# Query and key preparation by quarters of the heads in two buffers, with joint transfers, a matmul mask for the maxima, and new orders

## The reference

```python
q = _rmsnorm((x @ Wq).reshape(B, T, H, D), q_rms_w)
k = _rmsnorm((x @ Wk).reshape(B, T, H, D), k_rms_w)
v = (x @ Wv).reshape(B, T, H, D)
omega_eff = softplus(omega) * slopes
gate = softplus(einsum('bthd,hd->bht', k, u_n) / sqrt(D))   # one factor per key and head
bias = -dist * omega_eff * gate            # dist = max(i - j, 0)
bias = where(causal, bias, -inf)
attn = softmax(q @ k.T / sqrt(D) + bias)
y = (attn @ v).reshape(B, T, H * D) @ Wproj
```

## Time and profile before

| | |
|---|---|
| median of 3 runs | 910.95 us (905.34 to 912.75) |
| the profiled execution | 906.46 us, span 904.7 us |
| mean granted TensorE clock of it | 0.954 |
| busy: PE, DVE, ACT, POOL | 784.6, 701.8, 652.3, 646.0 us |
| DMA bytes | 77.92 MB, 96,546 packets |

### The profile page before, as it was taken

How to read it: one execution, slowest core, us unless ns; L and a number is a source line. 1 busy time by engine, 2 the same in 40 slices (tenths; PEclk the granted TensorE clock), 3 DMA queues, 4 the chain that set the end, 5 groups by cost and what they waited for, 6 DMA issues and landing times.

```text
span 904.7 us, 25206 instructions
## 1 busy us (share of the span) xinstructions
PE 784.6 (87%) x9336; PEld 539.2 (60%) x9336; DVE 701.8 (78%) x2230; ACT 652.3 (72%) x1401; POOL 646.0 (71%) x746
## 2 busy tenths in 40 slices
PE   2548988898999999898998999998998899998974
PEld 1233755576666676576665776576665766575752
DVE  7868858786878879687876879787877879798933
ACT  5555857675996789766986879866986779863643
POOL 2523856687698868788697868889697868884761
PEclk9687999999999999999998999999999999999986
DMA  7033623647044711746054630746054720826330
GB/s 200 4 68 75 137 42 60 119 83 131 2 109 93 172 32 35 143 97 131 2 122 74 157 52 14 162 96 135 2 117 85 158 45 14 164 56 136 49 60 12
DMA packets 96546, 77.92 MB, mean 86 GB/s; under 512 B 72982, under 2 KB 83432, under 8 KB 96360
## 3 DMA queue, kind: packets, MB, share of 16 engines
q1 hardware_dynamic: 95912, 74.72, 40.6%
q10 hardware_dynamic: 512, 1.59, 0.8%
HBM read 5.29 MB, written 2.10 MB: 8 GB/s over the span
## 4 chain that ended last, share of the span: by engine, by line
PE 46%; SPq 13%; ACT 10%; DVE 9%; DMA 9%; issue 6%; POOL 5%; ACTq 0%; DVEq 0%; POOLq 0%
PE ps L955 10%; PE ps L957 9%; PE ps L956 9%; SPq L595 8%; PE ps L1059 5%; SPq L599 4%; PE ps L1074 3%; DMA y_hl<-ytt 3%; PE ps L1100 3%; PE ps L1101 3%; DMA k<-gtt 3%; ACT qkn L898 3%; DMA k<-qkn 3%; POOL qkn L777 3%; DVE junk L1359 2%
## 5 line engine op out<-in xcount | busy, mean ns | idle before, releaser
L753 POOL TENSOR_TENSOR pt_l<-pt 128x512 f16<-128x512 f32 x368 | 320.8, 901 | 112.7 <-ACT pt L928 112.6
L1359 DVE CUSTOM_DVE_ANT_0 junk<-ps,causal_row 128x512 f16<-128x512 f32 (+3 forms) x512 | 219.3, 486 | 46.5 <-PE ps L1074 45.3
L928 ACT ACTIVATE pt<-ps 128x512 f32<-128x512 f32 (+1 forms) x384 | 176.7, 527 | 71.0 <-PE ps L1102 46.4
L777 POOL TENSOR_TENSOR qkn<-qkn,rs 128x512 f32<-128x512 f32 x124 | 128.5, 1067 | 57.3 <-ACT rs L866 57.3
L1100 PE MATMUL ps<-q,k 128*128 128x512 f16 (+3 forms) x512 | 148.2, 302 | 1.0 <-ACT pt L928 0.7
L1101 PE MATMUL ps<-q,k 128*128 128x512 f16 (+3 forms) x512 | 147.5, 301 | 0.0
L955 PE MATMUL ps<-v_buf,pt 128*128 128x65 f16 x1280 | 131.8, 195 | 2.1 <-DVE ytok L1380 1.5
L1074 PE MATMUL ps<-k,q 96*128 96x512 f16 (+3 forms) x512 | 98.9, 306 | 38.9 <-DMA k<-gtt 24.8
L956 PE MATMUL ps<-v_buf,pt 128*128 128x65 f16 x1280 | 131.7, 194 | 0.0
L957 PE MATMUL ps<-v_buf,pt_l 128*128 128x65 f16 x1280 | 131.4, 194 | 0.0
L955 PEld LDWEIGHTS ps<-v_buf,pt 128*128 128x128 bf16 x1280 | 118.9, 98 | 14.4 <-issue 5.8
(11 more groups left out here) (178 smaller groups left out, 1994.6 us busy)
## 6 DMA issues: line engine op xcount, KB each, us to landing
q<-qkn SPq DMA_DIRECT2D x96, 256.0 KB, 5.2
k<-qkn SPq DMA_DIRECT2D x90, 256.0 KB, 5.9
x_in<-in_L_attn_x SPq DMA_DIRECT2D x8, 256.0 KB, 3.2
out<-x_out SPq DMA_DIRECT2D x8, 256.0 KB, 2.3
k<-qkn ACTq DMA_DIRECT2D x6, 256.0 KB, 8.2
k<-q SPq DMA_DIRECT2D x1, 1024.0 KB, 9.2
q<-nmt SPq DMA_DIRECT2D x64, 2.0 KB
y_hl<-ytt SPq DMA_TRANSPOSE x64, 3.3
```

Of the source, the lines that this page charges most:

```text
L753: g.tensor_tensor(pt_l[:, h % 2, c], pt[:, h % 2, c], pt_h[:, h % 2, c], ALU.subtract).then_inc(s_pt_l, 1)
L777: g.tensor_tensor(qk, qk, r.unsqueeze(3).broadcast_to([P, HH // 2, 2, D]), ALU.mult).then_inc(s_qkn, 1)
L928: a.activation(pt[:, h % 2, c], ps[:, j, 0:width], ACT.Exp).then_inc(s_exp, 1)
L1359: ins = d.tensor_tensor_reduce(junk[:, part.unit(s, i)[0], col:col + (ib + 1) * P], part.bank(s, i)[:, col:col + (ib + 1) * P], causal_row ...
```

## The change

1. **Quarters, two buffers.** `qk` is now (quarter `qd`, block `t`): one bank holds four heads of q and four of k. There are 16 such banks a batch as before, in two places of `qkn` of four heads each, used in turn; the whole is as large as before. `take_qk` waits for the transfers of the quarter before the last one only.
2. **Joint transfers.** `q1`, `k1` become one tensor `qk1` with, per quarter and odd or even heads, a block of k beside a block of q; `q2`, `k2` become `qk2`. The parts in `qkn` lie so that a transfer carries a q and a k block. A quarter takes 2 DMAs for the upper parts of `qk1`, 2 for the gate rows (four rows by two heads each), 4 for `qk2`. The bytes are the same, and so is the number of DMAs of a batch (32). Maxima wait for their quarter's first four DMAs. In batch 0 ACT issues the odd heads' part of quarters 0 and 1 (`place_odd_heads`), three 256 KB DMAs each.
3. **Mask by matmul.** Behind each of the four matmuls of a head's maxima PE adds the mask with a 128-column matmul; DVE takes the maximum with a plain `tensor_reduce` that negates and writes 16-bit numbers. `nm` turns and copies 16-bit numbers. The buffer `junk` is gone.
4. **Heads and weights.** Heads are computed in an order in which pairs are swapped (`pair_of`, `head_of`); Wq and Wk are loaded in 8 pieces so that the weights lie by quarters. The scale of the gate logits moves into two ACT instructions. POOL's `over_rms` waits once for two blocks, and does both of them, 16 of 512 elements a batch as before; in batch 0 DVE does the keys of quarters 0 and 1.
5. **New orders** on all engines, in all parts but `tail`.

```diff
-UNITS = {"m": 2, "h": 4, "out": 1, "qk": 2, "gl": 1, "gr": 1, "t": 2, "a": 3, "nm": 1, "v": 1, "wp": 1}
+UNITS = {"m": 2, "h": 4, "out": 1, "qk": 1, "gl": 1, "gr": 1, "t": 2, "a": 3, "nm": 1, "v": 1, "wp": 1}
...
+        def uses(b, qd):
+            return (b * 4 + qd) // 2 + 1
+        def place_upper(eng, qd, n):
+            eng.dma_start(qk1[0:D, qd, n, :, :, :], qkn16[n * D:(n + 1) * D, qd % 2, 1:3, :, :]).then_inc(s_upper[qd % 2], 16)
+        def place_lower(eng, qd, n):
+            eng.dma_start(qk2[D:P, qd, n, :, :, :], qkn16[n * D:(n + 1) * D, qd % 2, 0:2, :, :]).then_inc(s_low[qd % 2], 16)
+            eng.dma_start(qk2[0:D, qd, n, :, :, :], qkn16[n * D:(n + 1) * D, qd % 2, 2:4, :, :]).then_inc(s_low[qd % 2], 16)
...
+            def place_operands(part, s, b, qd):
+                both = range(1) if b == 0 and qd < 2 else range(2)
+                sp.wait_ge(s_hi, b * H + (qd + 1) * QH)
+                for n in both:
+                    place_upper(sp, qd, n)
+                part.taken(sp, ("gr", qd // 2, s[-1]))
+                for n in range(2):
+                    sp.dma_start(qk1[GROW:GROW + 4, qd, n, 0, :, :],
+                                 gtt[qd % 2 * 2 + n::4, :]).then_inc(s_gates[qd % 2], 16)
+                part.taken(sp, ("t", 2 * qd + 1, s[-1]), 1)
+                for n in both:
+                    place_lower(sp, qd, n)
...
+            def take_qk(part, s, b, qd, t):
+                if t == 0 and b * 4 + qd >= 2:
+                    act.wait_ge(s_upper[qd % 2], (uses(b, qd) - 1) * 32)
+                    act.wait_ge(s_low[qd % 2], (uses(b, qd) - 1) * 64)
...
             def max_scores(part, s, b, h):
-                pe.wait_ge(s_grow, (b * 2 + h // HH + 1) * 128)
+                pe.wait_ge(s_upper[qd % 2], uses(b, qd) * 32)
+                pe.wait_ge(s_gates[qd % 2], uses(b, qd) * 32)
...
-                        mm = pe.matmul(dst, q1[0:MROW, row(h), ib * P:keys], k1[0:MROW, row(h), 0:keys], start=True, stop=True)
+                        pe.matmul(dst, q1(h)[0:MROW, ib * P:keys], k1(h)[0:MROW, 0:keys], start=True, stop=False)
+                        mm = pe.matmul(dst[:, ib * P:keys], ident16[:, :], causal16[:, :], start=False, stop=True)
...
             def maxima(part, s, b, h):
-                        ins = d.tensor_tensor_reduce(junk[:, part.unit(s, i)[0], col:col + (ib + 1) * P], part.bank(s, i)[:, col:col + (ib + 1) * P],
-                                                     causal_row[:, T - (ib + 1) * P:T], 1.0, -3.0e38, ALU.add, ALU.max,
-                                                     negm[:, ib, column(h):column(h) + 1])
+                        ins = d.tensor_reduce(negm[:, ib, h:h + 1], part.bank(s, i)[:, col:col + (ib + 1) * P], AX.X, ALU.max,
+                                              negate=True)
...
             def take_max_rows(part, s, b, qd):
-                part.taken_by(d.tensor_scalar(nmt[:, :], part.bank(s)[0:QH, :], -1.0, None, ALU.mult), s)
+                part.taken_by(d.tensor_copy(nmt[:, :], part.bank(s)[0:QH, :].bitcast(F16)[:, 0:T]), s)
```

More of the change, by code:

```diff
@@ L489, in macaron @@
         s_out = sem("s_out")
-        s_dup = sem("s_dup")
-        s_low = sem("s_low")
-        s_grow = sem("s_grow")
+        s_upper = [sem(f"s_upper{i}") for i in range(2)]
+        s_low = [sem(f"s_low{i}") for i in range(2)]
+        s_gates = [sem(f"s_gates{i}") for i in range(2)]
         s_mrow = sem("s_mrow")
@@ L712, in _ @@
             for h, s in enumerate(slopes_of(H)):
-                last = g.memset(slopes[:, row(h):row(h) + 1], s)
+                last = g.memset(slopes[:, h:h + 1], s)
             last.then_inc(s_const, 1)
@@ L839, in gelu @@
                 act.preload_act_table_set(EXP_SET)
-            def take_qk(part, s, b, hf, t):
-                g = b * 2 + hf
-                if t == 0 and g > 0:
-                    act.wait_ge(s_grow, g * 128)
-                    act.wait_ge(s_dup, g * 64)
-                if t == TB // 2 and g > 0:
-                    act.wait_ge(s_low, g * 64)
-                blk = g * TB + t
-                for j in range(2):
-                    part.full(act, s, j)
-                    if blk >= 2:
-                        act.wait_ge(s_sqsum, (blk - 2) * 2 + j + 1)
-                    a.activation(sq[:, t % 2, j, :], part.bank(s, j), ACT.Square).then_inc(s_sq, 1)
-                    part.taken_by(a.activation(qkn[:, j, t // 2, :, (t % 2) * P:(t % 2 + 1) * P],
-                                               part.bank(s, j).rearrange("p (i n) -> p i n", n=P), ACT.Copy), s, j)
@@ L864, in inverse_rms, with two @@
+            def inverse_rms(part, s, b, qd, th):
+                n = (b * 4 + qd) * 2 + th + 1
+                def two(t):
+                    return t[:, :, qd % 2, 2 * th:2 * th + 2, :].rearrange("p j t m -> p j (t m)")
+                act.wait_ge(s_sqsum, n * 2)
+                a.activation(two(ssl), two(ss), ACT.Ln, bias=rms_eps[:, :],
                              scale=1.0 / (D * QKV_UP * QKV_UP)).then_inc(s_ssl, 1)
-                act.wait_ge(s_ssl, blk + 1)
-                a.activation(rs[:, t, :], ssl[:, t, :], ACT.Exp, scale=-0.5).then_inc(s_rs, 1)
+                act.wait_ge(s_ssl, n)
+                a.activation(two(rs), two(ssl), ACT.Exp, scale=-0.5).then_inc(s_rs, 1)
@@ L897, in hi_parts, with place_odd_heads @@
                     part.full(act, s, j)
-                    a.activation(qkn16[:, j, 0, p % 4, :], part.bank(s, j), ACT.Identity, scale=w[:, :]).then_inc(s_hi, 1)
-            def place_first_keys(part, s, b, hf):
-                if b + hf == 0:
-                    act.wait_ge(s_k1_zero, 16)
-                    act.wait_ge(s_hi, HH)
-                    place(act, k1[0:D, :, :], 0, 1, 0, s_grow)
-                    part.taken(act, ("gr", *s[1:]))
-                    for r in range(2, 4):
-                        place_gates(act, 0, r)
-                    place(act, k2[D:P, :, :], 0, 1, 0, s_dup)
-                    part.taken(act, ("t", 3, s[-1]), 1)
-                    place(act, k2[0:D, :, :], 0, 1, 1, s_low)
+                    a.activation(qkn16[:, p // 2 % 2, UPPER[j], p % 2, :], part.bank(s, j), ACT.Identity, scale=w[:, :]).then_inc(s_hi, 1)
+            def place_odd_heads(part, s, b, qd):
+                if b == 0 and qd < 2:
+                    if qd == 0:
+                        act.wait_ge(s_k1_zero, 16)
+                    act.wait_ge(s_hi, (qd + 1) * QH)
+                    place_upper(act, qd, 1)
+                    part.taken(act, ("t", 2 * qd + 1, s[-1]), 1)
+                    place_lower(act, qd, 1)
             def v_hi(part, s, b, j, t):
```

593 lines of the change are left out of this document (307 added, 286 removed).

## The result

| | before | after |
|---|---|---|
| median of the runs (lowest to highest) | 908.14 us (904.37 to 912.75) | 834.42 us (833.35 to 835.25) |
| ratio, 95% interval | | 0.9185 (0.9133 to 0.9238) |
| span of the profiled execution | 904.7 us | 833.3 us |
| mean granted clock | 0.954 | 0.975 |

Times are medians of the fast runs, and a ratio is always to the kernel before, measured beside the run in question. The changed kernel is 8.1% faster.

What follows compares the result with a forecast made beforehand. PE, busy 784.6 of 904.7 us, was taken as the bound, with idle time hanging on the `qkn` buffer wait. 906.5 + 28.7 - 6.4 - 12.2 - 12.0 - 4.1 - 7.3 - 3.0 - 2.0 = 888.2, plus 2: 890 us, range 868 to 914.

Steps and rivals of the forecast that it cites:

- PE "busy 93.6": First body at full clock: PE busy for 93.6 of 99.0 us, taken as work that counts in full.
- I let 3.0 us stand: Bodies: of 5.4 us idle PE in a full-clock body, 3.0 us stay, so -2.4 x 5 = -12.0 us.
- bound to one buffer that no longer exists: Bodies: the projection's wait behind the first half's transfers hangs on the single `qkn` buffer and goes with two.
- Masks, +28.7: PE, all batches: 512 mask matmuls of 128 columns at 0.056 us each add 28.7 us, nothing hidden.
- Turns, -6.4: PE: four turns of the maxima take 0.40 us in 16 bits against 0.60; 32 blocks save 6.4 us.
- Maxima on DVE, 0: DVE: plain reduction takes about 1.2 ns a column, as the fused mask and maximum does, so no change.
- lead -6.1: Kernel start: -4.1 us from half the 8.2 us wait before the first maxima, -2.0 from moving DVE's low weight parts.
- 115 to 249 -7.3: Stretch 115 to 249 us: 4.0 of 5.0 us gate-row waits and half of 6.7 us low clock go, -7.3 us.
- late -3.0: Behind the last body's start: of 3.3 us of gate-row waits, 3.0 us go.
- Slower: the waits only move: Rival, bodies: PE waits for DVE's maxima instead of DMA, nothing won there, 925 us; chance 0.15.
- Only the clock comes back: Rival, no change: long waits go, short ones take their place, 907 us; chance 0.20.
- Faster still: Rival: idle PE falls to 1 us a body, outside stretches lose remaining low clock and waits, 871 us; chance 0.18.

Runs made afterwards that it cites:

- the model of before's wait: Changed kernel, copies of quarters 0 and 2 waiting for both buffers' upper halves and their own lower halves: 902.8 us with old orders, 854.9 us with new orders.

## Why the prediction was right and wrong, step by step

- **The steps that failed, and their sizes.** The sum gave 888.2 us for the profiled execution, which took 835.25: 53 us less. Three steps account for it. PE "busy 93.6", with 2.8 us for masks less turns (and 0.3 because the stretch read was 99.0 us long and the period 99.3), stood as a floor of 96.7 us a body, and was 94.2: 12.5 us in five bodies. The idle PE left in a body, "I let 3.0 us stand", was 0.4: 13 us. And outside the five bodies the sum had -8.1 us where -35.9 were measured: 28 us. So the terms of gain were too small everywhere, while the price of the masks as PE's work was right.
- **What bounds the kernel.** That the wait of the earlier trace rows would go with the clock's falls was right: the clock is 1.00 in every body. That PE "busy 93.6" is work that stays was wrong. Dense time was 87.0 us, so up to 6.6 us of the busy time were gaps too short to be seen in it; after the change the same difference is 4.2 us (94.2 and 90.0), so some 2.4 of them went. The page Perfetto Trace Analysis of the Trainium skill (Identifying the Most-Contended Engine) says that busy time of matmuls is no good measure of the headroom, since matmuls are pipelined; the traces agree, by these 6.6 us, and the prediction did not weigh it.
- **Idle PE after: "I let 3.0 us stand".** It was 0.4. The excess fell from 14.8 to 4.6 us, 51 us in five bodies, where the forecast had 12.2 + 12.0 = 24.2. In the busy times, the mean body's idle PE fell by 6.3 us (101.75 less 95.03, to 0.4) and its busy time beyond the dense one by 3.8 (8.0 to 4.2). The forecast kept more than half of the idle time of a full-clock body and all of the short gaps; the reordering took away both. I had written that "a new order always has waits of its own", with no row behind it.
- **Buffers as the cause.** The prediction gave the gain to the buffer ("bound to one buffer that no longer exists"). By the model of before's wait it is worth 4.6 us in the old orders; the new orders are worth 48 to 64 us, and they had no term of their own in the sum.
- **Masks, +28.7.** Right as PE's work (a mask's step is 0.056 us, the dense time grew by 22.9 us in all, and doubled masks cost 23.0), but their price in time depends on the kernel: in the kernel before, masks and turns together cost 3 us, where PE had 14.8 us of excess a body, and in the changed kernel removing the masks brings 9.8. "Nothing hidden, because PE is the fullest engine" was the wrong reason.
- **Turns, -6.4.** Measured 5.2 in the changed kernel (832.7 against 827.5), with the copy's part in it. Right.
- **Maxima on DVE, 0.** Right; the lines by form, first of after and then of before:

```profile
L1401 DVE TENSOR_REDUCE negm<-ps 128x1 f16<-128x512 f32 x128 | 88.0, 687 | 22.6 <-PE ps L1115 21.3
L1401 DVE TENSOR_REDUCE negm<-ps 128x1 f16<-128x384 f32 x128 | 70.4, 550 | 0.0
```

```profile
L1359 DVE CUSTOM_DVE_ANT_0 junk<-ps,causal_row 128x512 f16<-128x512 f32 x128 | 87.9, 687 | 42.7 <-PE ps L1074 41.5
L1359 DVE CUSTOM_DVE_ANT_0 junk<-ps,causal_row 128x384 f16<-128x384 f32 x128 | 70.7, 553 | 0.0
L1359 DVE DVE_READ_ACCUMULATOR2_ANT negm<- 128x1 f32 x512 | 42.4, 83 | 0.0
```

  687 ns are listed both ways, and in a row one starts 0.60 us (reduction) or 0.61 us (fused) after another, as the prediction named. What the page VectorE: DVE Perf Modes of the Trainium skill (Rules for kernel authors) says of `tensor_reduce` as the slowest operation does not hold against this fused one, which moreover brings 512 reads of the accumulator of 83 ns. These lie almost wholly under the instruction ahead: without them DVE would be busy for 701.4 us of the 701.8.
- **The stretches outside the bodies.** Forecast: lead -6.1, 115 to 249 -7.3, late -3.0, together -16.4, with 8.3 of masks less turns added -8.1. Measured: -23.8 and -12.1, together -35.9. The wait before the first maxima went wholly, not by half, and so did those for gate rows. The masks are there all the same: the dense time outside the bodies grew by 8.6 us, and the excess fell by 44.6 where the sum had 16.4. That is 18.6 us up to the second batch's first scaling of gate logits, 15.3 from there to the third's and 10.7 behind the last body's start (the orders also moved work into the first of these stretches). No run split the 44.6 by cause. `add` of the lead starts at 29.95, where it started at 32.81: 2.9 us for the 2.0 forecast; the low part of Wproj takes 1.22 us in its new place (23.70).
- **Rivals.** "Slower: the waits only move" is refuted as a whole: PE's matmuls wait for DVE's maxima once, 0.2 us, and its weight loads 20 times, 5.9 us over the whole span. DVE, though, is the engine that stands next: without masks DVE has 15% of the chain. "Only the clock comes back" is refuted by the excess. "Faster still", at 1 us of idle PE, was the nearest; it missed by 37 us, since it kept the busy floor and had 7.5 us more for the stretches outside where 28 more went.
- **The range** ended at 868: all cases shared the 93.6, and none had more than 24 us of gain outside the bodies.

## What to carry to other kernels

Before an engine's busy time is used as a floor, count its work start to start at the rate of its fastest stretches: of 93.6 us "busy", 87.0 were dense. That is a lower bound; the best kernels here stayed 4.5 us a body above it. In this kernel the second buffer was worth little without the new orders, and the orders lost their gain with one wait too many; cost them as one design, by asking how early the first consumer can start and what covers the next transfer. The price of added or removed work holds for one direction only: here doubling the masks cost 23 us, removing them gave 10, and adding them to a kernel full of waits cost 3. And before a step is moved because of a wait, make sure by counting which step it is that waits: two runs here acted on the wrong one.

## What the runs showed of the hardware

- One wait of 5.0 us on PE is followed by 4.5 us at half the clock with PE fully busy, so it costs 7.3. In the changed kernel no gap on PE in the bodies exceeds its dense step by more than 0.4 us, and the clock stays at 1.00.
- The reduction of 512 f32 columns from PSUM takes 687 ns, as long as the fused add-and-maximum of the same columns; the latter also has an accumulator read of 83 ns behind it, nearly all of it overlapped.
- The two durations of one kind of DVE instruction that the prediction read in the earlier trace rows also show after: the low part of a Wqkv piece took 2.29 us at 27.73 and 1.22 us at 34.16. The page SBUF — State Buffer of the Trainium skill (SBUF: two separate sides) says that a VectorE instruction with two SBUF inputs and a GpSimd instruction that reads SBUF exclude each other; the two durations fit that, and no run here separated the cause.
